# GpSimd's fourth y tile: adding the negated mean instead of subtracting the mean

## What is computed

```python
# layer 1: attention over edges of kind 1..4, scores h*a_k . h, leaky_relu, softmax
x = _layernorm(x + _L0_gnn_ref(x, adj, a_0, a_1, a_2, a_3))
# layer 2: relational graph convolution, (xW + b) * sigmoid(xW Wg + bg) summed over neighbours, relu
x = _layernorm(x + _L1_gnn_ref(x, nodemask, adj, W_*, Wg_*, b_*, bg_*))

def _layernorm(x, axis=-1, eps=1e-05):
    m = jnp.mean(x, axis=axis, keepdims=True)
    v = jnp.var(x, axis=axis, keepdims=True)
    return (x - m) / jnp.sqrt(v + eps)
```

## Time and profile before

| | us |
|---|---|
| median of 3 runs | 123.91 |
| lowest, highest | 122.56, 124.81 |
| the profiled execution's own time | 123.48 |
| its span in the trace | 121.6 |
| PE, DVE, ACT, POOL busy | 103.2, 92.2, 86.2, 90.2 |

### The profile page before, as it was taken

One profiled execution on the slowest core, in us unless ns is written; L12 is line 12 of the kernel. 1 busy time (PEld: TensorE's weight loads), 2 busy tenths in 40 slices (PEclk: granted clock), 3 DMA queues, 4 the chain that ended last, 5 costly groups with the idle time before them and its releaser, 6 DMA issues. The chain is left out here.

```text
span 121.6 us, 2570 instructions
## 1 busy us (share of the span) xinstructions
PE 103.2 (85%) x677; PEld 92.3 (76%) x684; DVE 92.2 (76%) x374; ACT 86.2 (71%) x198; POOL 90.2 (74%) x141
## 2 busy tenths in 40 slices
PE   6649595999999999999999999999999979489300
PEld 6638385999999989899898999999989868287100
DVE  0020956689999999999899999999999999627500
ACT  4478469798989898898989898989897583212000
POOL 4000060606999999899999999999999999998890
PEclk9999959999999999999999999999999999958975
DMA  1999999998556583838386020202020202111132
GB/s 35 313 322 297 289 290 289 295 293 215 177 172 204 146 234 111 254 112 248 103 242 171 4 86 8 86 0 86 0 86 6 86 18 71 35 54 53 33 94 89
DMA packets 34770, 17.36 MB, mean 143 GB/s; under 512 B 1217, under 2 KB 34754, under 8 KB 34754
## 3 DMA queue, kind: packets, MB, share of 16 engines
q1 hardware_dynamic: 34608, 17.17, 51.7%
q10 hardware_dynamic: 146, 0.00, 0.1%
HBM read 12.98 MB, written 4.19 MB: 141 GB/s over the span
## 5 line engine op out<-in xcount | busy, mean ns | idle before, releaser
L799 PE MATMUL p_hg<-w_both,y_t 128*128 128x256 f32 x128 | 31.7, 391 | 1.3 <-ACT y_t L615 1.3
L799 PEld LDWEIGHTS p_hg<-w_both,y_t 128*128 128x128 f32 x128 | 23.4, 193 | 4.9 <-ACT w_both L611 1.5
L654 DVE CUSTOM_DVE_ANT_0 nscore<-p_e,rel 128x128 f32<-128x128 f32 x64 | 14.7, 284 | 12.0 <-ACT rel L590 11.7
L623 ACT ACTIVATE th<-p_hg 128x256 f32<-128x256 f32 x32 | 12.3, 383 | 12.1 <-PE p_hg L799 11.2
L538 POOL TENSOR_TENSOR out_s<-cent,rs 128x256 f32<-128x256 f32 x32 | 18.9, 613 | 2.5 <-issue 0.5
L598 ACT ACTIVATE prob<-nscore,nmax 128x128 f32<-128x128 f32 x64 | 20.3, 393 | 0.0
L509 POOL TENSOR_SCALAR rs<-st 128x4 f32<-128x4 f32 x16 | 3.1, 194 | 21.5 <-DVE st L676 21.5
L668 DVE SCALAR_TENSOR_TENSOR res<-p_o,rz,inputs 128x128 f32<-128x128 f32 x64 | 18.0, 345 | 0.6
L810 PE MATMUL p_ag<-vals,mask 128*128 128x128 f32 x128 | 18.2, 286 | 0.2 <-DVE vals L697 0.2
L746 PEld LDWEIGHTS p_e<-inputs,xat 128*128 128x128 f32 x128 | 17.5, 199 | 0.7
L746 PE MATMUL p_e<-inputs,xat 128*128 128x128 f32 x128 | 17.5, 281 | 0.5 <-issue 0.2
(11 more groups left out here) (53 smaller groups left out, 147.8 us busy)
## 6 DMA issues: line engine op xcount, KB each, us to landing
inputs<-x_t SPq DMA_DIRECT2D x16, 256.0 KB, 4.7
inputs<-adj SPq DMA_DIRECT2D x16, 256.0 KB, 5.0
inputs<-x SPq DMA_DIRECT2D x16, 256.0 KB, 5.2
out<-out_s SPq DMA_DIRECT2D x15, 256.0 KB, 2.3
out<-out_s SPq DMA_DIRECT2D x2, 128.0 KB, 2.1
w_rows<-w SPq DMA_DIRECT2D x1, 192.0 KB, 4.6
wg_s<-wg_t SPq DMA_DIRECT2D x1, 192.0 KB, 4.6
a_col<-a ACTq DMA_DIRECT2D x1, 0.5 KB, 3.0
```

Of the source, the lines that this page charges most:

```text
L654: nc.vector.tensor_tensor_reduce(nscore[:, k, i], p_e[:, i], rel4[:, k, i], -SLOPE, FLOAT_MAX, ALU.add, ALU.min, nmax[:, k, i:i + 1]).then ...
L799: last = nc.tensor.matmul(p_hg[:, i], y_t[:, g % 2, i], w_both[:], start=True, stop=True)
```

## The change

GpSimd gets one more instruction in `norm1`: a pass over one column (128x1) multiplies the mean of the fourth graph by -1 into a new tile `minus1`. The y of the fourth graph then adds `minus1` and multiplies, where it subtracted the mean and multiplied. A new semaphore makes y wait for the pass. VectorE's three y tiles stay as they were.

```diff
+        minus1 = sb("minus1", [P, 2, 1])
+        minus1_done = sem("minus1_done")
@@ norm1
                 nc.gpsimd.tensor_scalar(rs1[:, k, 0], st1[:, k, :, 2], 1.0 / P, EPS, ALU.mult, ALU.add)\
                     .then_inc(var1_done, 1)
+                nc.gpsimd.tensor_scalar(minus1[:, k], st1[:, k, G - 1, 1:2], -1.0, None, ALU.mult)\
+                    .then_inc(minus1_done, 1)
                 pool.wait_ge(var1_done, g + 1)
                 if g >= 2:
                     pool.wait_ge(y_done, 3 * (g - 1))
                 nc.gpsimd.tensor_tensor(rs1[:, k, 1], rs1[:, k, 0], minus_half[:], ALU.pow).then_inc(rstd1_done, 1)
+                pool.wait_ge(minus1_done, g + 1)
                 pool.wait_ge(rstd1_done, g + 1)
                 if g >= 4:
                     pool.wait_ge(r2_done, g - 3)
                     pool.wait_ge(ty_done, g - 3)
-                nc.gpsimd.tensor_scalar(y[:, g % 4, G - 1], res1[:, k, G - 1], st1[:, k, G - 1, 1:2],
-                                        rs1[:, k, 1, G - 1:G], ALU.subtract, ALU.mult).then_inc(y3_done, 1)
+                nc.gpsimd.tensor_scalar(y[:, g % 4, G - 1], res1[:, k, G - 1], minus1[:, k],
+                                        rs1[:, k, 1, G - 1:G], ALU.add, ALU.mult).then_inc(y3_done, 1)
```

## The result

The changed kernel takes 130.06 us (128.8 to 132.41, 4 runs); the kernel before takes 123.77 beside it. The ratio is 1.051, with a 95% interval of 1.036 to 1.066. It is slower by 5%, where 2.4% faster was forecast. Some executions of these kernels run a per cent or two longer at a lower granted clock (the kernel before beside e1: 122.28 us at 0.966, 124.57 at 0.939); a median is over all executions, a ratio over the others alone. The profiled execution took 129.52 us with a span of 127.7, 6.1 longer than before.

What follows compares the result with a forecast made beforehand. POOL was taken to bound the late turns at 5.89 us, above a 5.75 floor. Shorter turns gave 2.25 us and the drain's clock 0.3, together 2.55, from 123.48 to 120.9 us; range 119.9 to 125.2.

Steps and rivals of the forecast that it cites:

- What bounded the kernel: Steady turns: POOL sets the late ones of 5.89 us; ScalarE and the gate matmuls close the early ones.
- a floor of 5.75: ScalarE and gate matmul loop without POOL or y: 5.75 us under any POOL change, winning 0.14 at most per late turn.
- the sum: Whole kernel: POOL's turn 5.39, steady turns 5.75; 2.25 us won by the last L509 plus 0.3 in the drain, together 2.55.
- y: GpSimd's y of the fourth graph, adding: 0.3 us alone, about 0.5 beside L687, from 1.05, a gain of 0.55.
- The comparison with L529: Subtraction in L529 costs no more per element than multiplication in L538, 1.7 ns; speaks against subtraction making y slow.
- The pass: Added 128x1 pass on POOL between L509 and L514: 0.05 us taken, from a possible 0.03 to 0.15.
- The wait: Wait on `minus1_done` ahead of `rstd1_done`: costed at nothing, covered by L514's 1.01 us; uncovered 0.08 to 0.11.
- The step that failed: Steady turns: POOL's own turn becomes 5.39, under the floor, so turns fall to 5.75 and POOL waits for `stats1`.
- The rival on contention: VectorE's L687 beside GpSimd's y: new y gains only 0.2, less 0.05 for the pass; 122.3 us, chance 0.12.
- The rival that ends slower: Pass on POOL holds L514 back by the full 0.27 for 12 to 15 turns, no y gain; 127.5 us, chance 0.09.
- no gain in y: GpSimd's y stays at 1.05 and the pass adds 0.05 per POOL turn; +1.2, 124.7 us, chance 0.24.
- the clock in the drain: Shorter wait for y at the end lifts part of the low clock: 0.3 us, a third of about 0.9 in matmuls.

Runs made afterwards that it cites:

- e1: The kernel before with the added pass over the mean and its wait, but y still subtracting the mean itself; 127.82 us, ratio 1.039.
- e8: The kernel before, fourth graph's y adding the un-negated mean (sign changed, no pass), cent waiting for VectorE's y of the group two ahead; 121.64 us, ratio 0.9925.
- e4: The changed kernel with one wait more: GpSimd's cent waits for VectorE's three y of the group two ahead; 122.41 us, ratio 1.000.
- e11: The kernel before with eight extra 128x128 instructions ending GpSimd's list, VectorE idle; subtract and multiply 0.80 us, add and multiply 0.45; total not compared.
- e10: The changed kernel with the negation on VectorE instead of GpSimd, and cent waiting for VectorE's y of the group two ahead; 121.8 us, ratio 0.988.
- e12: The changed kernel with GpSimd's cent (128x512) cut into two instructions of 128x256, nothing moved; 125.61 us, ratio 1.021.
- e6: The changed kernel with the pass behind the power and cent waiting for VectorE's y of the group two ahead; 124.5 us, ratio 1.017.
- e9: The kernel before with only the wait of cent on VectorE's y of the group two ahead; 124.68 us, no interval.

## Why the prediction was wrong

*What bounded the kernel.* Right: POOL set the late turns, and the loop of ScalarE and TensorE is a floor of 5.75; e8 runs at it. The forecast of 2.4% sets a time worked out from the profiled execution against the median; the 2.55 us of the sum are 2.1% of that execution's 123.48.

*y.* Right in size, 0.45 against 0.5, and partly by luck. The 0.5 was for a y beside L687 and 0.3 for one alone; measured are 0.64 beside it (e4) and 0.45 alone. And from y's start to the next instruction's the gain is 0.50, not 0.60: that one starts 0.08 after y's end, where it started 0.02 before it. Wrong in the reasoning. I took 0.80 for a y partly held by VectorE, and estimated 0.43 for it alone. It is 0.80 alone (e11); the gain is the form itself, 0.35. The comparison with L529, in which subtraction is cheap, said nothing about this instruction.

*The pass.* Wrong: 0.05 taken. From the first norm1 instruction to the power it is now 0.46 (66.97 to 67.43) against 0.27, so 0.19. That is over the 0.03 to 0.15 that I had worked out and under the 0.27 of a full serialisation: the pass starts 0.27 after L511, not 0.15.

*The wait.* I costed it at nothing under the power. From the power to y it is 1.22 against 1.12: 0.10. In e10, which has the wait without the pass, it is 1.18 to 1.19, so most of it is the wait's own. POOL's own turn is then 0.27 + 0.19 + 1.22 + 0.53 + 0.15 + 1.05 + 1.18, and 1.15 for the last, 5.74, not the 5.39 of the sum. That alone would still have been just under the floor.

*The step that failed.* "POOL's own turn becomes 5.89 - 0.55 + 0.05 = 5.39, under the floor of 5.75, so the steady turns fall to 5.75 and POOL waits for `stats1`." The wait for `stats1` came true, and it made the turn of 5.75 false. The sum took VectorE's work to stay as it was, so it put the cost of GpSimd's earlier cent to VectorE at nothing; the runs show 0.81 us a turn. I followed the freed time up to GpSimd's own wait and didn't ask what GpSimd does next, sooner, and beside what. Cent comes 2.36 after the first norm1 instruction (66.97 to 69.33), which now starts when the statistics are ready, while VectorE's y starts 1.86 after the same instruction (66.97 to 68.83) and would take 0.92. The times for both were in the trace: VectorE's y started at 35.85 and cent at 36.48, overlapping by 0.25 already. That was 0.63 after it; now it is 0.50 (68.83 to 69.33), and cent issues just ahead of the third y.

*The rival on contention.* It looked at the other side, at whether VectorE slows GpSimd. What I set against it was the early y, which ended at 36.36 in the middle of L687. That y was not held at all: it issued before VectorE's first and took the 0.80 that it takes alone (e11). VectorE as the second behind cent was held: 1.13 beside a cent of 1.08, and 0.70 beside a half of 0.65 (e12), each ending some 0.15 after it. Behind GpSimd's y it differs. Behind the subtracting one VectorE isn't held: its three took 0.88 at 35.85 although y had been issued at 35.56. Behind the adding one, in the changed kernel, VectorE's first y takes 0.41 in place of 0.35 and ends 0.14 after GpSimd's y (69.24 against 69.10); in e10, where GpSimd's y was issued 0.09 after VectorE's first, VectorE's second and third, issued while it ran, take 0.34 each. For GpSimd as the second, y is compared with the 0.45 that it takes alone, or 0.80 before (e11). It loses 0.19 in e4, where 0.22 of VectorE's first were left when it was issued, and 0.25 before, where 0.28 were left; a wait for that one instruction would fit both. But it loses 0.49 in e10, more than the 0.25 that were left, and only 0.13 in e6, where nearly all of the third, 0.33, was left. So e6 speaks against the rival, by a y of 0.58 that was issued with the third and ended at 72.56, 0.24 after it; the early y of 0.80, with which I had argued, doesn't. No run tells what sets the size of the loss.

*The rival that ends slower* had its bound right (POOL) and its time nearly: e1 shows 127.82 where 127.5 stood, though a turn grew by 0.36, with the wait in it, and not by 0.27. It isn't what happened in the changed kernel. The rival "no gain in y" is out: y gained, and e11 shows that the pair of operations in the instruction changes its price.

*What stays open.* Why the pass starts 0.27 after L511, where L529 started 0.15 after L525, wasn't tried. What e9's wait costs has no interval. No run took an operand out of SBUF, so it is shown which instructions hold each other up and for how long, but not that it is their SBUF operands. The 0.3 us that I gave to the clock in the drain were my estimate and weren't put to the test either, and no run shows that the wait for y lowers the clock. There the eight L810 took 1.92 against 1.07 in a steady turn (from 69.70) and the eight L799 2.23 against 1.94, together 1.14 more, where I had about 0.9. In the changed kernel TensorE waits 1.38 and then 0.72 for y at the last transposes, against 2.20 before, and the granted clock is 1.00 from the last L511 on (111.43 to 118.09), against 0.71 before, but the work in that stretch isn't the same.

## What to carry to other kernels

Where an engine is made faster, list its next instructions with their new start times, and lay them over those of the other engines that may be held up beside it, above all those that have no slack; an engine that was late may have been keeping out of the way. If freed time turns into a wait of the faster engine while the total grows, look for an untouched engine whose instructions became longer. The remedy was cheap here: a wait that holds the long instruction back until the tight engine is through (e4, e8), or cutting it in pieces (e12), and with the pass off GpSimd too the short y was then worth 1.2% (e10).

## What the runs showed of the hardware

- GpSimd's tensor_scalar over 128x128 in f32 took 0.45 us for add then multiply, 0.80 for subtract then multiply, and 0.605 to 0.610 for a single add or subtract (e11).
- VectorE's y, issued 0.11 us after GpSimd's cent (1.08), ended 0.16 after it: 1.13 in place of about 0.35. Behind GpSimd's y in the subtracting form its three took 0.88, so it wasn't held (before, early turn); behind the adding form its first took 0.41 and ended 0.14 after that y (the changed kernel). The other way round GpSimd's y, issued while VectorE's three run, loses 0.13 (e6), 0.19 (e4), 0.25 (before) or 0.49 (e10).
- A 128x1 pass isn't nothing: 0.19 on GpSimd's way to the power, 0.39 in length where VectorE's y runs (e6), 0.14 to 0.15 on VectorE (e10).
